# Node biases as products of a row of ones, a fused multiply-sum for places, deep scores summed on ScalarE, and value chunks after the fourth transposes

## What is computed

```python
x = x + gnn(layernorm(x), h_neigh, adj, adj, Wq, bq, Wk, bk, Wv, bv, Wo, bo, E)
h = layernorm(x)                                   # 512 x 128
for level in range(8):                             # current starts at node 0
    score = (h * w1s[current]).sum(-1) + b1s[current]
    choice = ((sign(score) + 1) / 2).astype(int)   # right where the score is above 0
    logits.append(score); nodes.append(current)
    current = 2 * current + choice + 1
weight = gelu(abs(logits), approximate=False)
out = sum(weight[:, i] * (h @ w2s[nodes[i]] + b2s[nodes[i]]) for i in range(8))
x = x + out
```

## Time and profile before

| | |
|---|---|
| median of 3 runs | 141.93 us (140.77, 141.93, 142.02) |
| the profiled execution | 140.57 us |
| its span, first to last instruction | 138.8 us |
| mean granted TensorE clock in it | 0.977 of full |
| PE / PEld / DVE / ACT / POOL busy | 111.7 / 78.6 / 99.0 / 64.1 / 38.9 us |

### The profile page before, as it was taken

The page is one execution under the profiler, slowest core; times in us unless marked ns, Lnnn a source line. Parts: engine busy times, 40 slices in busy tenths (PEclk is TensorE's granted clock), DMA queues, the critical chain, the costliest instruction groups (busy, mean ns, idle before and its releaser), DMA issues.

```text
span 138.8 us, 3461 instructions
## 1 busy us (share of the span) xinstructions
PE 111.7 (80%) x995; PEld 78.6 (57%) x996; DVE 99.0 (71%) x292; ACT 64.1 (46%) x133; POOL 38.9 (28%) x83
## 2 busy tenths in 40 slices
PE   6998988389999999879898799589899659678800
PEld 2367743255565565555635364579888558667800
DVE  1788899978778888726898997235655786865660
ACT  3065297577977697621470044334434323343410
POOL 6483000000000000002200028344636426856552
PEclk9999999999999999999999999968999999999995
DMA  3985999999990000049970001100000000100000
GB/s 101 311 287 171 453 453 439 427 397 415 434 448 19 7 0 5 0 149 409 398 297 19 0 0 43 38 0 0 0 2 0 2 0 0 38 5 0 0 19 19
DMA packets 3420, 20.15 MB, mean 145 GB/s; under 512 B 465, under 2 KB 2000, under 8 KB 2896
## 3 DMA queue, kind: packets, MB, share of 16 engines
q1 hardware_dynamic: 2048, 18.42, 32.6%
q10 hardware_dynamic: 1104, 1.05, 2.5%
q0 software_dynamic: 256, 0.52, 1.3%
HBM read 19.47 MB, written 0.52 MB: 144 GB/s over the span
## 4 chain that ended last, share of the span: by engine, by line
PE 30%; DVE 23%; issue 10%; DVEq 9%; ACT 7%; POOL 1%; ACTq 0%
PE turn_ps L661 9%; DVE early L1099 6%; DVEq L90 4%; DVEq L85 4%; PE s_ps L604 4%; PE s_ps L801 3%; ACT prob L465 3%; PE misc_ps L623 2%; DVE x L1114 2%; PE s_ps L543 2%; PE turn_ps L801 2%; DVE token_path L1018 2%; DVE prob L1059 2%; ACT w L461 1%; ACT prob_t L461 1%
## 5 line engine op out<-in xcount | busy, mean ns | idle before, releaser
L394 POOL TENSOR_TENSOR early<-early,scaled_sb 128x128 f32<-128x128 f32 x48 | 21.2, 456 | 21.4 <-ACT scaled_sb L526 18.7
L801 PE MATMUL s_ps<-w,msg 128*128 x128 | 19.5, 295 | 7.3 <-issue 3.3
L465 ACT ACTIVATE prob<-prob,negmax 128x512 f32<-128x512 f32 x32 | 21.7, 714 | 6.5 <-DVE negmax L975 6.5
L661 PE MATMUL turn_ps<-ident,prob 128*128 128x128 f32 x128 | 20.6, 284 | 3.3 <-ACT prob L465 2.0
L975 DVE CUSTOM_DVE_ANT_0 prob<-s_ps,mask 128x512 f32<-128x512 f32 x32 | 21.0, 685 | 2.5 <-PE s_ps L604 1.9
L801 PEld LDWEIGHTS s_ps<-w,msg 128*128 128x128 f32 x128 | 16.5, 199 | 9.9 <-issue 9.9
L1099 DVE SCALAR_TENSOR_TENSOR early<-s_ps,coef,early 128x128 f32<-128x128 f32 x48 | 14.3, 347 | 8.4 <-PE s_ps L801 4.4
L661 PEld LDWEIGHTS turn_ps<-ident,prob 128*128 128x128 f32 x128 | 13.5, 140 | 11.2 <-ACT prob L465 9.4
L371 POOL TENSOR_TENSOR rstd<-veps,mhalf 128x2 f32<-128x2 f32 x2 | 1.4, 715 | 54.0 <-DVE veps L835 54.0
L526 ACT ACTIVATE scaled_sb<-s_ps,coef 128x128 f32<-128x128 f32 x16 | 5.9, 368 | 15.3 <-PE s_ps L801 13.6
L543 PE MATMUL s_ps<-count_row,ones_h 128*128 128x512 f16 x52 | 12.7, 379 | 0.0
(11 more groups left out here) (184 smaller groups left out, 193.7 us busy)
## 6 DMA issues: line engine op xcount, KB each, us to landing
w<-in_w_t SPq DMA_DIRECT2D x3, 4096.0 KB, 22.8
w<-in_w_t SPq DMA_DIRECT2D x1, 4032.0 KB, 14.4
w<-in_adj SPq DMA_DIRECT2D x1, 1024.0 KB, 9.5
w_sb<-in_w_t ACTq DMA_DIRECT2D x1, 384.0 KB, 4.6
x_sb<-in_x SPq DMA_DIRECT2D x1, 256.0 KB, 3.3
msg<-in_neigh_t SPq DMA_DIRECT2D x1, 256.0 KB, 4.4
x_rows<-x ACTq DMA_DIRECT2D x1, 256.0 KB, 10.4
row_sb<-in_rows ACTq DMA_DIRECT2D x1, 255.5 KB, 8.3
```

Source lines behind the costliest of these rows:

```text
L394: nc.gpsimd.tensor_tensor(mine, mine, scaled_sb[:, i, :], ALU.add).then_inc(pooled[i], STEP)
L465: nc.scalar.activation(prob[:, u % RING, :], prob[:, u % RING, :], ACT.Exp, bias=negmax[:, t, h:h + 1], scale=-1.0).then_inc(exped, 1)
L661: last = nc.tensor.transpose(turn_ps[u % 2][:, m * P:(m + 1) * P], prob[:, u % RING, m * P:(m + 1) * P], ident[:])
L801: nc.tensor.matmul(product_ps[j], hs_t[:, s * P:(s + 1) * P], w2_flat[:, bass.ds(found[j], D)], start=True, stop=True).then_inc(multiplied ...
```

## The change

Six edits. (1) A row of ones is made on GpSimd; TensorE multiplies it with the row of node biases into `s_ps`, four products with one row of weights each, and the node products then add to that. The fillers there go from eleven to four. (2) VectorE compares straight from PSUM, and neither of its bias additions is left; the product with the path reads PSUM too. (3) Product and sum for `pos` become one fused instruction for each tile. (4) The sums of the two deepest levels move to ScalarE, eight activations with an accumulated output, which wait for the product with the path (`prod_ready`) and stand ahead of the absolute value in ScalarE's program. (5) VectorE's level sums go from eight to six. (6) Value chunks 2 and 3 of a quad stand behind the transposes of place 3, where they stood ahead of them.

```diff
             nc.gpsimd.iota(token_path[:, :, 0], [[P, TILES]], base=0, channel_multiplier=1,
                            allow_small_or_imprecise_dtypes=True).then_inc(consts2, 1)
+            nc.gpsimd.memset(ones_row[:], 1.0).then_inc(consts2, 1)
...
+            act.wait_ge(prod_ready, 1)
+            for l, room in ((DEPTH, x_sb), (DEPTH - 1, h_sb)):
+                n = 2 ** l
+                for t in range(TILES):
+                    nc.scalar.activation(room[:, t, 0:n], prod[:, t, n - 1:2 * n - 1], ACT.Copy,
+                                         accum_out=picked[:, t, l:l + 1]).then_inc(deep_picked, 1)
+            act.wait_ge(deep_picked, 2 * TILES)
             act.wait_ge(picked_ready, 1)
...
-                if quad > 0 and place == 3:
-                    weighted_values(quad - 1, 2)
-                    weighted_values(quad - 1, 3)
                 if u >= 14 and (u - 14) % HEADS == 0:
                     values_back((u - 14) // HEADS)
                 pe.wait_ge(exped, u + 1)
...
                 if u == 2:
                     scores(QUAD, QUAD + 2)
+                if quad > 0 and place == 3:
+                    weighted_values(quad - 1, 2)
+                    weighted_values(quad - 1, 3)
...
-            pe.wait_ge(consts2, 10)
+            pe.wait_ge(consts2, 11)
...
+            pe.wait_ge(row_in, 16)
+            for t in range(TILES):
+                nc.tensor.matmul(s_ps[:, t // 2, (t % 2) * NODES_PAD:(t % 2) * NODES_PAD + NODES],
+                                 ones_row[:], row_sb[0:1, B1:], start=(t % 2 == 0), stop=False)
             for i, (t0, t1) in enumerate(GROUPS):
-                keep_busy((11, 3)[i])
+                keep_busy((4, 3)[i])
...
-                                            h_t[:, t * P:(t + 1) * P], w1_sb[:], start=True, stop=True)
+                                            h_t[:, t * P:(t + 1) * P], w1_sb[:], start=False, stop=(t == t1 - 1))
...
-                then(nc.vector.tensor_tensor(scores_b[:, t0:t1, 0:LEAF0], node_scores[:, t0:t1, 0:LEAF0],
-                                             b1[:, :, 0:LEAF0].to_broadcast([P, t1 - t0, LEAF0]), ALU.add))
-                nc.vector.tensor_scalar(sides[:, t0:t1, 0:LEAF0, 0], scores_b[:, t0:t1, 0:LEAF0], 0.0, None,
+                nc.vector.tensor_scalar(sides[:, t0:t1, 0:LEAF0, 0], node_scores[:, t0:t1, 0:LEAF0], 0.0, None,
                                         ALU.is_le)
...
-            then(nc.vector.tensor_tensor(scores_b[:, :, LEAF0:NODES], node_scores[:, :, LEAF0:NODES],
-                                         b1[:, :, LEAF0:NODES].to_broadcast([P, TILES, LEAVES]), ALU.add))
             dve.wait_ge(path_ready, 1)
-            then(nc.vector.tensor_tensor(prod[:, :, 0:NODES], scores_b[:, :, 0:NODES], path[:, :, 0:NODES],
-                                         ALU.mult))
+            nc.vector.tensor_tensor(prod[:, :, 0:NODES], node_scores[:, :, 0:NODES], path[:, :, 0:NODES],
+                                    ALU.mult).then_inc(prod_ready, 1)
             dve.wait_ge(placed, 1)
-            then(nc.vector.tensor_tensor(place_l, turn_ps[0][:].rearrange("p (t n) -> p t n", n=LEAVES),
-                                         path[:, :, LEAF0:NODES], ALU.mult))
-            then(nc.vector.tensor_reduce(pos[:], place_l, AX_X, ALU.add))
+            for t in range(TILES):
+                ins = nc.vector.tensor_tensor_reduce(out=place_l[:, t, :], in0=turn_ps[0][:, t * LEAVES:(t + 1) * LEAVES],
+                                                     in1=path[:, t, LEAF0:NODES], scale=1.0, scalar=0.0, op0=ALU.mult,
+                                                     op1=ALU.add, accum_out=pos[:, t:t + 1])
+            then(ins)
...
-            for l in range(LEVELS):
+            dve.wait_ge(prod_ready, 1)
+            for l in range(DEPTH - 1):
                 ins = nc.vector.tensor_reduce(picked[:, :, l], prod[:, :, 2 ** l - 1:2 ** (l + 1) - 1], AX_X, ALU.add)
             ins.then_inc(picked_ready, 1)
```

More of the change, by code:

```diff
@@ L155, in gnn_ffn_kernel @@
         ones_h = sb("ones_h", [P, P], F16)
+        ones_row = sb("ones_row", [1, P])
         before = sb("before", [P, P], F16)
@@ L223, in gnn_ffn_kernel @@
         nodes = row_room[0:1, :].bitcast(I32)
-        scores_b = view(mask[:], 0, TILES * NODES_PAD, F32, "p (t n) -> p t n", n=NODES_PAD)
         prod = prob_t[:].rearrange("p a n -> p (a n)").rearrange("p (t n) -> p t n", n=NODES_PAD)
@@ L287, in gnn_ffn_kernel @@
             sem("coef_turned"), sem("coef_t_ready"))
+        prod_ready, deep_picked = sem("prod_ready"), sem("deep_picked")
         x1_sorted = [sem(f"x1_sorted{t}") for t in range(TILES)]
```

5 lines of the change are left out of this document (2 added, 3 removed).

## The result

| | before | changed |
|---|---|---|
| median | 141.98 us (140.77 to 142.55, 4 runs) | 137.24 us (137.09 to 138.66, 4 runs) |
| profiled execution | 140.57 us | 138.66 us |
| its span | 138.8 us | 136.9 us |
| its mean granted clock | 0.977 | 0.964 |

The ratio is 0.969, with a 95% interval from 0.962 to 0.977. The two profiled executions are 1.9 us apart, the medians 4.7. That gap is the first thing to explain, and the clock under the spans is where to look.

The account below looks back on a forecast made before the run. No engine is full, so the chain of waits was taken as the bound. Savings of 0.40, 0.58 and 1.09 sum to 2.07: 138.5 us from the profile, 139.9 from the median; forecast 139.6, range 137.8 to 141.5.

Parts of the forecast that it names:

- the last step of the sum: Whole kernel: 138.5 us on the profile's scale or 139.9 on the median's; 139.6 chosen, between them and nearer the median.
- the sum of 2.07: All savings together: 0.40 in attention rounds, 0.58 at the attention's end, 1.09 up to the lists.
- The rival of a stretch gone or doubled: Slow-clock stretch in the node loops: gone, 138.0 us, chance 0.13; one more, 141.3 us, chance 0.08.
- Value chunks: Attention: chunks behind the fourth transposes save 0.08 at five starts of scores, 0.40, and 0.58 at the end.
- who feels that?: Attention rounds: VectorE's earlier fourth-head copy helps through its two masks, which open the next scores; 0.08 each.
- Bias products: Ahead of the node products: four products add at most 1.72, seven fewer fillers remove 1.50; waiting hides it, cost 0.
- The slower rival: Clock falls to 1.2 GHz under the bias products from 64 us through the node products: 144.9 us, chance 0.05.
- Comparisons: Ahead of the path: two comparisons from PSUM take 0.75 instead of 1.00; gain 0.23, between 0.15 and 0.46.
- Fused sums and fillers: Places to lists: fused sums take 0.95, twelve fillers limit the count product's gain to 0.37; lists 1.09 earlier.
- Deep sums: Eight level sums on idle ScalarE take 3.2, done before the split needs them: cost 0.

Follow-up runs that it names:

- two bridged runs: Two of twelve runs of the kernel before with only eight fillers added ahead of the third group of scores: 141.0 and 141.1 us; that kernel's median 140.77, ratio 0.993.
- Fewer fillers: Changed kernel with six fillers instead of twelve ahead of the count product: 137.07 us, ratio 0.967.
- the unfused version: Changed kernel with product and sum of the places as two instructions over four tiles again: 137.82 us, ratio 0.972.
- The bridge and fewer fillers: Changed kernel with six fillers for twelve ahead of the counts, eight added ahead of the third scores, three fewer around sorting and lists: 136.71 us, ratio 0.963.
- two passes: Bridged six-filler changed kernel, its one-row bias products done twice with weights of 0.5, none of the four fillers behind them: 136.66 us, ratio 0.979.

## Why the prediction was wrong

**The scale.** Two steps failed, the scale and the size of one term. The first is the last step of the sum: "between the two scales and nearer the median". I had one profile, at 140.57, and a median of 141.93, and could "only partly place" the gap. The runs place it. Most mean clocks of a kernel lie near 0.99, 0.975, 0.964 or 0.952, and the times go with them, with exceptions like the two bridged runs above: the unedited changed kernel took 136.3 at 0.990, 137.3 and 137.4 at 0.975, 138.4 at 0.964, 138.7 and 139.3 at 0.952. One fit over 103 runs on the three chips of the first rounds of experiments, with one slope for all kernels, gives 0.8 us per 0.01 of mean clock. In the profiles each level down is one more stretch of 3.4 us at 1.2 GHz (none at 0.987, one at 0.977, two at 0.961 to 0.965, three at 0.952; two stretches in direct sequence gave 0.959 and 0.962). The kernel before took 140.1 to 141.2 at 0.971 to 0.978 (14 of its first 36 runs) and 141.2 to 142.8 at 0.963 to 0.965 (14 more). By these levels its median is that of runs with two stretches, while its profile had one; and the four runs whose median is 137.24 had mostly one (three of them at 0.972 to 0.976). By the profile's scale my own sum said 138.5. The forecast missed by 2.4 us: 1.1 of them, from 138.5 to 139.6, were spent on a scale to which the changed kernel didn't belong, and they put the time outside the range. The other 1.3 are terms: about 1.0 that the traces show and the sum of 2.07 lacked (0.6 in the attention, 0.15 up to the lists, 0.2 behind them), and 0.3 left over. At equal clock, 0.971 to 0.978, before takes 140.5 in the mean and the changed kernel 137.25: 3.3 us, 2.3%. The rest of the 4.7 between the medians is which runs were drawn, and that is luck.

The rival of a stretch gone or doubled had a chance of 0.21 together; it is the everyday state of both kernels. I had priced one at 1.6 to 1.8; measured, it costs 1.1 in the first round (5.58 against 4.49), 1.6 ahead of the path (12.92 against 11.31) and in the loops, from the second half of their first step to the end, 1.0 on one chip (48.9 against 47.9) and 0.2 on another (48.7 against 48.5). That such stretches come and go at one and the same program is now seen: the changed kernel's own profiles have them at 28 and 110 us in one, and at 108 us alone in the next. The Trainium skill (TensorE: Matmul & The Clock Gate, Part 1: The HAM clock gate) says that the clock's monitor runs freely and doesn't start again with the kernel; the traces agree with that, and don't test it.

**Value chunks.** Right that the transposes of the fourth head come first and the chain through ScalarE isn't shortened directly; the term was mis-sized, and it is the second step that failed. I asked "who feels that?" of VectorE's early copy, and named only the masks. The other is the next quad's second head, whose transposes go into the buffer that the copy empties; they stood 0.71 behind the first head's and now stand 0.61. So the 0.08 that TensorE waited ahead of the scores was no upper bound: TensorE had come there late itself, because of the same copy. I took 0.08 a round, 0.40 in all; it is 0.19 a round, and from the first round to the last group of scores about 0.9 in all (1.59 less the 0.66 of the end). At the end I took 0.58; it is 0.66. Together 1.6 against 0.98. As said, the scores start 0.58 behind the value products, not 0.66.

**Bias products.** Right: 1.98 for eight records (expected 1.89), TensorE still waits for the rows, nothing lost. The slower rival rested on the clock falling there at once and for good. It didn't in the changed kernel's profile; stretches did begin there in five others, each for 3.4 us, 1.6 us of time where the path could be compared, never near the 5 us that the rival needed. No run of a changed kernel was above 142.0, let alone 144.9.

**Comparisons.** Right. 0.45 and 0.34 apart, and the path started 0.27 earlier after the last value products, forecast 0.23. The row of a one-source read out of PSUM was the right neighbour, and the comparison of 0.31 out of SBUF the wrong one. That agrees with the Trainium skill (VectorE: DVE Perf Modes, section Why PSUM operands drop a tier), by which it was 0.23.

**Fused sums and fillers.** Right in mechanism, and 0.15 short in size. Four fused instructions took 0.97 from the first start to `from_tile` (forecast 0.95). The count product came 0.39 earlier (0.37), the copy of the counts 0.92 (0.85), the lists 1.24 (1.09). Fewer fillers and the unfused version bear out both halves: the fillers held the count product, and VectorE's gain there lay idle.

**Deep sums.** Right, cost 0: 2.2 us for eight (forecast 3.2) and off the path. Taking them from VectorE is what let TensorE bind before the lists; with them back on VectorE the wait of 0.26 returned.

**What is left over.** Terms read from the traces: 1.6 in the attention, 1.24 to the lists, another 0.2 between the lists and the second half of the loops' first step (30.49 to 29.06 after the last value products, 1.43 in all), together 3.0 of the 3.3. Of the 0.2, ScalarE's second copy is the place, and its cause is open. The last 0.3 is within the scatter of single runs at one clock level (140.3 to 141.2 for the kernel before on one chip).

No version here beats the changed kernel by more than its interval. The bridge and fewer fillers have the lowest ratio, 0.963 [0.956, 0.971], against 0.967 and 0.969.

## What to carry to other kernels

Before adding a sum of savings to a median, ask of the profile which state of the clock it was in, and put the forecast on the profile's own scale if the median can't be matched with it. When a copy comes earlier, follow both of its consequences: who reads what it wrote, and who overwrites what it read. A filler block that was matched to a wait must be cut with the wait, and then the next engine in line is what is left.

## What the runs showed of the hardware

- A product of 255 columns in fp32 shows as two records, and takes about 0.24 us a record with one row of weights (eight in 1.98, and sixteen in 3.70 with two passes) and with 128 (eight in 1.89).
- A sum with an accumulated output on ScalarE costs 0.29 to 0.31 us for 128 elements and 0.24 for 64, and a read of 0.19 beside it; the pairs follow each other at 0.29 and 0.24, so the read is nearly hidden. VectorE's fused product and sum takes 0.29 for 128 elements with a read of 0.08, 0.21 apart.
- The same kernel on two chips started the second half of its loops' first step 1.4 us apart (27.11 and 28.48 after the last value products). The kernel before had a median of 139.6 on one chip and 140.6 to 141.9 on others; at mean clocks of 0.971 to 0.978 it took 139.4 there and 140.5 to 140.7 on the others. On one and the same chip its median was 141.9 at one time and 140.63 at another. Times of different chips are compared here by their ratios to the kernel before; the clock levels alone are pooled, over three chips on which that kernel's medians lay within 0.7 us (141.24 to 141.91) when the fit's runs were made.
